# Mamba layer and exact-weight MLP on one core: the second part's first-gelu rows taken ahead, and its first block prepared beside the tail of the first part

## The chip, the cores and the metric

The kernel runs on one core of one Trainium2 chip. The metric is the device time of one execution in microseconds; three runs of the kernel before are given, and one more execution was recorded by the profiler. TensorE is called PE, VectorE DVE, ScalarE ACT, GpSimd POOL, SyncE SP. Only SP issues the DMAs that matter here.

## The reference

The input is x of shape (4, 2048, 256), float32. Two residual layers follow each other:

```
x = x + mamba(layernorm(x))          # conv of 4 taps, scan over 16 states, gate, 512 -> 256
h = silu(n @ w1 * s1) * (n @ w2 * s2)   # n = layernorm(x), 256 -> 1024, weights -1, 0, 1
h = gelu(h @ h1 * t1)                # 1024 -> 1024
h = gelu(h @ h2 * t2)                # 1024 -> 1024
x = x + (h @ w3) * s3                # 1024 -> 256
```

Since the weights of the MLP are -1, 0 or 1, the kernel may split each activation into a part rounded to float32r ("high") and the rest ("low"), and multiply both by the weights with two fast matmuls; a flag, computed early, says whether all weights have few enough bits for that. If they have, all engines take the branch `exact()`, otherwise `general()`. With the given inputs it is `exact()`.

## The kernel before, in words

**First part.** The 8192 rows are cut into 32 chunks (CHUNKS) of 256 rows. A chunk passes through stages norm, front, scan, post and mlp, and one body of the program (`bodies`, `stages`) works on several chunks at once: the scan of chunk c, beside it post of c-1 and the four quarters of mlp of c-1 to c-4. Tables PE_AT, DVE_AT, ACT_AT, POOL_AT and SP_AT say at which step of a body each engine does a piece. The mlp stage ends with h1: PE writes a pair of its output rows into one of three shared PSUM banks (L1380), ACT copies them to the tile z_out (two buffers, L775), and SP stores them to the DRAM tensor z_scratch (L549). The next job may use the bank when ACT has taken it. ACT waits before it fills a z_out buffer until the store of what was in it has landed. `ending` (L407) runs the four bodies that are left after the last scan: post of chunk 31 and the last mlp quarters. In it PE does the h1 matmuls (L1380) and the w1/w2 matmuls (L1369; jobs ug0 to ug7 of a chunk, one bank each). ACT takes the tanh of each ug job (L917), DVE gates it with two instructions (L1089, L1093) and so frees the bank, and after two of them ACT rounds (L924) and POOL subtracts (L761).

**Second part, `exact()`.** Each engine first waits in `pass_a_over` (L498) for all stores of the first part. Then come 16 blocks (CB) of 512 rows. Of a block, SP loads z from z_scratch in two DMAs of 1 MB to zb (two buffers, `load_z`, L619); ACT takes gelu of its 8 rows (`first`, L973) into the 4-deep ring wide; DVE splits each row into act_high and act_low (`split_first`, two instructions, L1173 and L1175); PE multiplies by h2 in 8 jobs of 16 matmuls (`second_layer`, L1415), each job into one of 8 banks; ACT takes the second gelu from the bank, into wide again (`second`, L980); DVE splits that row into act2_high and act2_low (`split_second`, L1173 and L1175 too); and PE multiplies by w3 in 64 matmuls (`last_layer`, L1427). `last_layer` of block b-1 stands after three h2 jobs of block b (W3_AFTER). DVE scales the result, adds x1 and so ends the block (`finish`, L1193 and L1199), and SP stores it.

The order on ACT is second(b, o), first(b+1, o) for o from 0 to 7. On DVE it is finish(b-1), then split_second(b, o), split_first(b+1, o). The split of the second gelu of row 0 waits until last_layer(b-1) has read act2. PE starts block b when all its 8 first rows are split. The first block has no such preparation in front of it: its load, its 8 gelus and its 8 splits all come after `pass_a_over`.

Of the kernel before, what the change touches and what calls it, by code (L numbers as in the profile page):

```python
# [38 lines left out]
def program(nc, x, w_in, conv_w, conv_b, w_x, w_dt, b_dt, a_log, d_skip, w_out,  # L39
# [25 lines left out]
    with ExitStack() as ctx:  # L65
# [37 lines left out]

        w_out_sb = sb("w_out_sb", [P, ET, DIM], where=a_only)
# [18 lines left out]
        dt = sb("dt", [P, 2, ET, T], where=a_only)  # L123
        u = sb("u", [P, ET, T], where=a_only)
        b_row = sb("b_row", [P, 2, QUARTER, T], where=a_only)
        b_first = sb("b_first", [P, NS], where=a_only)
        ub = sb("ub", [P, 2, ET, T], where=a_only)
        h = sb("h", [P, 2, ET, T], where=a_only)
# [33 lines left out]
        zb = sb("zb", [P, 2, KH, TB], where=b_only)  # L162
        wide = sb("wide", [P, WIDE, TB], where=b_only)
        xr = sb("xr", [P, 2, NTB, DIM], where=b_only)
# [6 lines left out]
        act_high = sb("act_high", [P, 2, KH, TB], F32R, where=b_only)  # L171
        act_low = sb("act_low", [P, 2, KH, TB], F32R, where=b_only)
# [245 lines left out]
        z_in = [sem(f"z_in{n}") for n in range(2)]  # L418
        xr_in = [sem(f"xr_in{n}") for n in range(2)]
        gelu1_ready = sem("gelu1_ready")  # L420
        high_ready = sem("high_ready")
        rows_split = sem("rows_split")
# [6 lines left out]
        W3_AFTER = 3  # L429

# [8 lines left out]

        def first_row(blk, o):  # L440
            return o if blk == 0 else KH + 2 * KH * (blk - 1) + 2 * o + 1

        def second_row(blk, o):
            return KH + 2 * KH * blk + (2 * o if blk < CB - 1 else o)
# [74 lines left out]
        def _(sp):  # L519
# [67 lines left out]
            for c in range(CHUNKS):  # L587
                to_norm, to_front, to_post, to_mlp = stages(c)
                for n in range(NS):
                    if n == SP_AT["x"] and to_norm is not None:  # L590
                        load_x(to_norm)
                    if n == SP_AT["write_b"] and to_front is not None:
                        write_b(to_front)
                    for quarter in (2, 3):
                        if n == SP_AT["b"][quarter]:
                            read_b(c, quarter)
                    for quarter in (0, 1):
                        if n == SP_AT["b"][quarter] and to_front is not None:
                            read_b(to_front, quarter)
                    if to_post is not None:  # L600
                        post(to_post, n)
                    for k in reversed(range(MLP_BODIES)):
                        if to_mlp[k] is not None:
                            mlp(to_mlp[k], NS * k + n)
                    if c == CHUNKS - 1 and n == 2:
                        sp.wait_ge(u_ready, CHUNKS)
                        sp.wait_ge(job_full, filled["acc1", CHUNKS - 1] + 1)
                        sp.wait_ge(xn_ready, CHUNKS)
                        sp.wait_ge(b_written, 32 * CHUNKS)
                        for name, src in (("h2", h2), ("w3", w3)):  # L610
                            sp.dma_start(again[name][:], src.rearrange("(k p) n -> p k n", p=P)).then_inc(late_in, 16)
            ending(post, mlp, NS)
            pass_a_over(sp)

            def exact():
                def load_z(blk):
                    after(sp, gelu1_ready, KH * (blk - 1))
                    for half in range(2):
                        sp.dma_start(zb[:, blk % 2, :, half * T:(half + 1) * T], z_dram[2 * blk + half]).then_inc(z_in[blk % 2], 16)  # L619

                def load_rows(blk):
                    after(sp, out_e_ready, blk - 1)
                    sp.dma_start(xr[:, blk % 2], x1_rows_b[:, blk]).then_inc(xr_in[blk % 2], 16)

                load_z(0)
                load_z(1)
                load_rows(0)
                load_rows(1)
                for blk in range(CB):
                    if blk + 2 < CB:  # L630
                        load_z(blk + 2)
                    sp.wait_ge(out_e_ready, blk + 1)
                    sp.dma_start(out_rows[:, blk], out_e[:, blk % 2]).then_inc(out_e_stored[blk % 2], 16)
                    if blk + 2 < CB:
                        load_rows(blk + 2)
                for slot in range(2):
                    sp.wait_ge(out_e_stored[slot], 8 * CB)

            def general():
# [17 lines left out]

                for name, src in (("w1", w1), ("w2", w2), ("h1", h1), ("h2", h2), ("w3", w3)):
                    sp.dma_start(whole_w[name][:], src.rearrange("(k p) n -> p k n", p=P)).then_inc(whole_in, 16)
# [109 lines left out]
        def _(act):  # L769
# [31 lines left out]
            def with_logs(to_front, to_norm, to_mlp):  # L801
# [12 lines left out]
                nc.scalar.preload_act_table_set("exp_and_others")  # L814
# [151 lines left out]
            ending(post, mlp, ACT_STEPS)  # L966

            def exact():
                def first(blk, o):
                    row = first_row(blk, o)  # L970
                    after(act, rows_split, row - WIDE + 1)
                    act.wait_ge(z_in[blk % 2], 32 * (blk // 2 + 1))
                    nc.scalar.activation(wide[:, row % WIDE], zb[:, blk % 2, o], ACT.Gelu, scale=scales[:, 2, o:o + 1]).then_inc(gelu1_ready, 1)  # L973

                def second(blk, o):
                    row = second_row(blk, o)
                    job = ("h2", blk, o)
                    after(act, rows_split, row - WIDE + 1)
# [52 lines left out]
        def _(dve):  # L1031
# [137 lines left out]
            ending(post, mlp, DVE_STEPS)  # L1169

            def exact():
                def split(row, blk, high, low, first_in_layer):
                    nc.vector.tensor_copy(high, wide[:, row % WIDE]).then_inc(high_ready, 1)  # L1173
                    dve.wait_ge(high_ready, row + 1)
                    nc.vector.tensor_tensor(low, wide[:, row % WIDE], high.bitcast(F32), ALU.subtract).then_inc(rows_split, 1)  # L1175

                def split_first(blk, o):
                    dve.wait_ge(gelu1_ready, KH * blk + o + 1)
                    if o == 0 and blk >= 2:
                        dve.wait_ge(e_full, e_place["h2", blk - 2, KH - 1] + 1)  # L1180
                    split(first_row(blk, o), blk, act_high[:, blk % 2, o], act_low[:, blk % 2, o], o == 0)

                def split_second(blk, o):
                    e_taken(dve, ("h2", blk, o))
                    if o == 0 and blk >= 1:
                        dve.wait_ge(e_full, e_place["out", blk - 1, NTB // 2 - 1] + 1)
                    split(second_row(blk, o), blk, act2_high[:, o], act2_low[:, o], o == 0)
# [75 lines left out]
        def _(pe):  # L1263
# [139 lines left out]
            def exact():  # L1403
                def free(job):
                    k = e_place[job]
                    after(pe, e_free[k % E_RING], k // E_RING)
                    return e_bank(job)

                def second_layer(blk, o):
                    into = free(("h2", blk, o))  # L1410
                    if o == 0:
                        pe.wait_ge(rows_split, first_row(blk, KH - 1) + 1)
                    for k in range(KH):
                        for part in (act_high, act_low):
                            last = nc.tensor.matmul(into, rounded["h2"][:, k, o * P:(o + 1) * P], part[:, blk % 2, k],  # L1415
                                                    start=(k == 0 and part is act_high), stop=(k == KH - 1 and part is act_low))
                    last.then_inc(e_full, 1)

                def last_layer(blk):
                    pe.wait_ge(rows_split, second_row(blk, KH - 1) + 1)  # L1420
# [10 lines left out]
                pass_a_over(pe)  # L1431
# [96 lines left out]
```

## Time and profile before

| | us |
|---|---|
| median of 3 runs (lowest, highest) | 3020.08 (3018.89, 3022.86) |
| the profiled execution, its own time | 3020.71 |
| its span, first to last instruction | 3018.9 |
| PE busy | 2677.9 (89%) |
| DVE busy | 2488.2 (82%) |
| ACT busy | 1831.0 (61%) |
| POOL busy | 1847.4 (61%) |

The profiled execution takes 1.8 us more than its span, and 0.6 us more than the median. The first part fills the span to about 2316 us, the second the 703 us that follow. Engines are named with the source line (L1415 is line 1415). "idle before" names the instruction that ended an idle stretch. PEclk is the granted clock of TensorE as a share of full speed; full speed is 2.4 GHz, and the other level is 1.2 GHz.

### The profile page before, as it was taken

The numbers are of one execution on the slowest core, as the hardware profiler recorded it, in microseconds if no ns is written. First come the engines' busy times: TensorE is split into PE (matmuls) and PEld (weight loads), VectorE is DVE, ScalarE is ACT, GpSimd is POOL, SyncE is SP. The second block draws the span as 40 slices with busy tenths as digits, with TensorE's granted clock in tenths as the row PEclk, the third lists the DMA queues.
The fourth block names the chain that finished last, engine by engine and source line by source line (L and its number), as shares of the span: only waits on it lengthen the run. The fifth ranks groups of instructions, "written<-read, shape, count | busy, mean of one in ns | idle before, by whom it ended". The sixth has DMA issues, their size and how long they took to land. (4 is left out here: it accounts for less than half of the span.)

```text
span 3018.9 us, 49123 instructions
## 1 busy us (share of the span) xinstructions
PE 2677.9 (89%) x17026; PEld 2350.8 (78%) x17026; DVE 2488.2 (82%) x3488; ACT 1831.0 (61%) x3488; POOL 1847.4 (61%) x1549
## 2 busy tenths in 40 slices
PE   5578999999999989999999989999876999999998
PEld 4457888888888878888888888888766787778777
DVE  4999999999999999999999999999962443454434
ACT  4667777777777777777777777777653222222221
POOL 3688888888888888888888888888841000000000
PEclk8799999999999999999999999999988999999999
DMA  6011111211212112211211112121213121222210
GB/s 212 22 50 47 54 54 58 71 61 54 70 55 61 54 54 60 68 61 54 71 54 61 54 54 65 63 61 55 95 66 125 60 82 44 84 84 84 76 51 29
DMA packets 130155, 198.78 MB, mean 66 GB/s; under 512 B 16368, under 2 KB 93296, under 8 KB 129904
## 3 DMA queue, kind: packets, MB, share of 16 engines
q1 hardware_dynamic: 129904, 195.57, 20.7%
q8 instruction: 140, 2.29, 0.3%
q14 instruction: 111, 0.91, 0.1%
HBM read 144.68 MB, written 50.86 MB: 65 GB/s over the span
## 5 line engine op out<-in xcount | busy, mean ns | idle before, releaser
L1107 DVE TENSOR_TENSOR_SCAN h<-banks,ub 128x512 f32<-128x512 f32 x1024 | 1192.1, 1205 | 42.2 <-POOL ub L738 28.9
L738 POOL TENSOR_TENSOR ub<-u,b_row 128x1020 f32<-128x1020 f32 x512 | 1214.0, 2371 | 0.3 <-issue 0.2
L1392 PE MATMUL banks<-ident,h 128*128 128x128 f32 x4096 | 608.8, 280 | 206.0 <-DVE acc L1120 195.4
L954 ACT ACTIVATE banks<-dt,neg_a 128x510 f32<-128x510 f32 x1024 | 683.8, 681 | 142.7 <-DVE h L1107 142.6
L1120 DVE SCALAR_TENSOR_TENSOR acc<-banks,c_tok,acc 128x512 f32<-128x512 f32 x1024 | 714.1, 736 | 5.8 <-PE banks L1392 4.8
L1392 PEld LDWEIGHTS banks<-ident,h 128*128 128x128 f32 x4096 | 473.9, 143 | 294.5 <-issue 126.7
L1380 PE MATMUL banks<-act_high,h_rounded 128*128 128x256 f32 x2048 | 533.3, 297 | 0.0
L1380 PE MATMUL banks<-act_low,h_rounded 128*128 128x256 f32 x2048 | 506.5, 283 | 0.0
L1415 PE MATMUL banks<-act_high,h_rounded 128*128 128x512 f32 x1024 | 419.3, 409 | 71.1 <-DVE act_low L1175 71.1
L1415 PE MATMUL banks<-act_low,h_rounded 128*128 128x512 f32 x1024 | 415.8, 406 | 0.0
L1380 PEld LDWEIGHTS banks<-act_low,h_rounded 128*128 128x128 f32 x2048 | 393.8, 192 | 0.0
L1380 PEld LDWEIGHTS banks<-act_high,h_rounded 128*128 128x128 f32 x2048 | 392.1, 191 | 0.0
L980 ACT ACTIVATE wide<-banks,scales 128x512 f32<-128x512 f32 x128 | 88.1, 689 | 484.9 <-PE banks L1415 292.6
L1415 PEld LDWEIGHTS banks<-act_high,h_rounded 128*128 128x128 f32 x1024 | 203.7, 199 | 120.7 <-issue 77.1
L1369 PE MATMUL banks<-xT_high,w_rounded 128*128 128x256 f32 x1024 | 272.0, 299 | 10.1 <-ACT z_out L775 9.1
L1193 DVE TENSOR_TENSOR prod_e<-banks,s_row 128x512 f32<-128x512 f32 x32 | 22.1, 692 | 312.6 <-PE banks L1427 312.6
L761 POOL TENSOR_TENSOR act_low<-wide,act_high 128x512 fp32r<-128x512 f32 x128 | 165.1, 1290 | 160.6 <-ACT act_high L924 160.6
L1369 PE MATMUL banks<-xT_low,w_rounded 128*128 128x256 f32 x1024 | 255.3, 282 | 0.0
L1303 PE MATMUL banks<-xp,conv_diag 128*128 128x256 f32 x1024 | 243.1, 380 | 0.0
L1415 PEld LDWEIGHTS banks<-act_low,h_rounded 128*128 128x128 f32 x1024 | 203.6, 199 | 43.1
L737 POOL TENSOR_TENSOR ub<-b_u,enter 128x4 f32<-128x4 f32 x512 | 104.8, 205 | 182.4 <-DVE h L1107 174.1
L1369 PEld LDWEIGHTS banks<-xT_high,w_rounded 128*128 128x128 f32 x1024 | 195.0, 190 | 17.4 <-ACT z_out L775 9.3
(111 smaller groups left out, 4257.0 us busy)
## 6 DMA issues: line engine op xcount, KB each, us to landing
b_row<-b_scratch SPq DMA_DIRECT2D x128, 512.0 KB, 3.9
z_scratch<-z_out SPq DMA_DIRECT2D x128, 256.0 KB, 5.0
zb<-z_scratch SPq DMA_DIRECT2D x32, 1024.0 KB, 9.0
x_sb<-in_x SPq DMA_DIRECT2D x32, 256.0 KB, 5.4
x_res<-in_x SPq DMA_DIRECT2D x32, 256.0 KB, 4.5
h_full<-in_h SPq DMA_DIRECT2D x2, 4096.0 KB, 17.9
x_scratch<-x_sb SPq DMA_DIRECT2D x32, 256.0 KB, 2.2
xr<-x_scratch SPq DMA_DIRECT2D x16, 512.0 KB, 5.8
```

The lines of the kernel that those rows point to most:

```text
L737: nc.gpsimd.tensor_tensor(ub[:, n % 2, :, 0], b_u[:, n], enter[:, n], ALU.add).then_inc(ub_ready, 1)
L738: nc.gpsimd.tensor_tensor(ub[:, n % 2, :, 1:], u[:, :, 1:], b_row[:, n // QUARTER % 2, n % QUARTER:n % QUARTER + 1, 1:].to_broadcast([P, E ...
L761: nc.gpsimd.tensor_tensor(act1_low[:, c % 2, 2 * p:2 * p + 2], wide1[:, p % 2], act1_high[:, c % 2, 2 * p:2 * p + 2].bitcast(F32), ALU.sub ...
L954: nc.scalar.activation(decay_half(k)[:, :, 1:], dt[:, par, 2 * i:2 * i + 2, 1:], ACT.Exp, scale=neg_a[:, n:n + 1]).then_inc(decay_ready, 1)
L980: nc.scalar.activation(wide[:, row % WIDE], e_bank(job), ACT.Gelu, scale=scales[:, 3, o:o + 1]).then_inc(e_free[e_place[job] % E_RING], 1)
L1107: nc.vector.tensor_tensor_scan(h[:, n % 2, 2 * i:2 * i + 2].rearrange("p e t -> p (e t)"), banks[:, k % DECAYS, :], ub[:, n % 2, 2 * i:2 * ...
L1120: nc.vector.scalar_tensor_tensor(out=acc[:, par, q], in0=turned[q], scalar=c_tok[:, par, q, n:n + 1], in1=acc[:, par, q], op0=ALU.mult, op ...
L1303: last = nc.tensor.matmul(into[:, i * T:(i + 1) * T], conv_diag[:, e, tap], xp[:, e, tap:tap + T], start=(tap == 0), stop=(tap == TAPS - 1))
L1369: last = nc.tensor.matmul(into[:, j * T:(j + 1) * T], weights[:, d, o * P:(o + 1) * P], rows[:, d], start=(d == 0 and rows is xT_high), st ...
L1380: last = nc.tensor.matmul(into[:, i * T:(i + 1) * T], rounded["h1"][:, k, o * P:(o + 1) * P], rows[:, c % 2, k], start=(k == 0 and rows is ...
L1392: last = nc.tensor.transpose(turned[q][:, e * P:(e + 1) * P], h[:, n % 2, e, q * P:(q + 1) * P], ident[:])
L1415: last = nc.tensor.matmul(into, rounded["h2"][:, k, o * P:(o + 1) * P], part[:, blk % 2, k], start=(k == 0 and part is act_high), stop=(k ...
```

## The change

- The tiles. `zb` is replaced by three tiles zl[0..2], taken in turn by block number modulo 3. The gelu is computed in place, and act_low[0..2] are in the same memory as zl[0..2]: DVE rounds the row to act_high (two tiles, block number modulo 2) and subtracts in place. The ring wide is left to the second gelu alone. zl[0] lies on memory of the scan's tiles, which are free when the last scan is over; zl[1] and zl[2] lie on the rounded weights of the first part, which are free when its last matmul is over. For that, five tiles of the scan (dt, u, b_row, ub, h) are declared earlier.
- The order of the second part. On ACT first(b+1, o) stands ahead of second(b, o), on DVE split_first(b+1, o) ahead of split_second(b, o), and finish(b-1) comes behind split_second(b, 3) instead of at the head of the block. One semaphore for all splits becomes one for the first and one for the second rows.
- The first block. SP issues the load of zl[0] ahead of `ending`, once the scan is over. ACT takes its 8 gelus and DVE its 8 splits in body 33 (the second of the four bodies of `ending`), at each fourth step of ACT's 32 and each sixth of DVE's 48. ACT loads the function table of gelu at its last change of table in the first part, instead of at the head of the second.
- The waits. PE no longer waits in `pass_a_over`, but for the rounded late weights (h2, w3) and the last scan's sums; where block 0 writes into one of the three shared banks, it waits for that bank. SP loads zl[1] and zl[2] after the last matmul of the first part. Later loads wait for the last h2 job of the block three before.

```diff
-        def ending(post, mlp, steps):
+        def ending(post, mlp, steps, first_rows=lambda c, n: None):
...
                     if to_post is not None:
                         post(to_post, n)
+                    first_rows(c, n)
...
+        FIRST_ROWS = [(CHUNKS + 1, 4 * o) for o in range(KH)]
...
+            def load_z(blk):
+                for slot in range(2):
+                    sp.wait_ge(z_stored[slot], 16 * PAIRS // 2 * 2 * (blk + 1))
+                for half in range(2):
+                    sp.dma_start(zl[blk % 3][:, :, half * T:(half + 1) * T], z_dram[2 * blk + half]).then_inc(z_in[blk % 3], 16)
+
+            sp.wait_ge(scan_done, 2 * NS * CHUNKS)
+            for q in range(NT):
+                sp.wait_ge(turn_full[q], NS * CHUNKS)
+            sp.wait_ge(carry_ready, NS * CHUNKS - 2)
+            load_z(0)
             ending(post, mlp, NS)
-            pass_a_over(sp)
...
-                load_z(0)
+                wait_full(sp, f"h{PAIRS - 1}", CHUNKS - 1)
                 load_z(1)
+                load_z(2)
+                pass_a_over(sp)
...
                 for blk in range(CB):
-                    if blk + 2 < CB:
-                        load_z(blk + 2)
+                    if blk + 3 < CB:
+                        sp.wait_ge(e_full, e_place["h2", blk, KH - 1] + 1)
+                        load_z(blk + 3)
...
-                    with_logs(None, None, c)
+                    with_logs(None, None, c, "gelu_and_others" if c == CHUNKS - 1 else "exp_and_others")
...
+            def first(blk, o):
+                act.wait_ge(z_in[blk % 3], 32 * (blk // 3 + 1))
+                nc.scalar.activation(zl[blk % 3][:, o], zl[blk % 3][:, o], ACT.Gelu, scale=scales[:, 2, o:o + 1]).then_inc(gelu1_ready, 1)
...
                 pass_a_over(act)
-                for o in range(KH):
-                    first(0, o)
                 for blk in range(CB):
                     for o in range(KH):
-                        second(blk, o)
                         if blk + 1 < CB:
                             first(blk + 1, o)
+                        second(blk, o)
...
+            def split_first(blk, o):
+                rows, high = zl[blk % 3][:, o], act_high[blk % 2][:, o]
+                dve.wait_ge(gelu1_ready, KH * blk + o + 1)
+                if o == 0 and blk >= 2:
+                    dve.wait_ge(e_full, e_place["h2", blk - 2, KH - 1] + 1)
+                nc.vector.tensor_copy(high, rows).then_inc(high1_ready, 1)
+                dve.wait_ge(high1_ready, KH * blk + o + 1)
+                nc.vector.tensor_tensor(act_low[blk % 3][:, o], rows, high.bitcast(F32), ALU.subtract).then_inc(split1, 1)
...
                 pass_a_over(dve)
-                for o in range(KH):
-                    split_first(0, o)
                 for blk in range(CB):
-                    if blk >= 1:
-                        finish(blk - 1)
                     for o in range(KH):
-                        split_second(blk, o)
                         if blk + 1 < CB:
                             split_first(blk + 1, o)
+                        split_second(blk, o)
+                        if o == W3_AFTER and blk >= 1:
+                            finish(blk - 1)
                 finish(CB - 1)
...
                     into = free(("h2", blk, o))
                     if o == 0:
-                        pe.wait_ge(rows_split, first_row(blk, KH - 1) + 1)
+                        pe.wait_ge(split1, KH * (blk + 1))
...
-                pass_a_over(pe)
+                pe.wait_ge(rounded_late, 10)
+                for q in range(NT):
+                    pe.wait_ge(y_added[q], NS * CHUNKS)
                 for blk in range(CB):
```

How the change moves the instructions is shown at three places.

**DVE, where block 1 ends and block 2 begins.** act and wide are first and second rows, the tiles called act2 belong to the second rows, prod_e and out_e to `finish`. Before:

```order
L1173 CAST act2_high<-wide 128x512
L1175 TENSOR_TENSOR act2_low<-wide,act2_high 128x512
L1173 CAST act_high<-wide 128x512
L1175 TENSOR_TENSOR act_low<-wide,act_high 128x512
L1193 TENSOR_TENSOR prod_e<-banks,s3_row 128x512 x2
L1199 TENSOR_TENSOR out_e<-prod_e,xr 128x1024
```

After the change, the same place two blocks on (zl1 is the block's own row 7, zl2 the next block's row 0):

```order
L1194 CAST act_high0<-zl1 128x512
L1196 TENSOR_TENSOR act_low1<-zl1,act_high0 128x512
L1210 CAST act2_high<-wide 128x512
L1212 TENSOR_TENSOR act2_low<-wide,act2_high 128x512
L1194 CAST act_high1<-zl2 128x512
L1196 TENSOR_TENSOR act_low2<-zl2,act_high1 128x512
```

The last first-row split, which PE waits for, now stands ahead of the last second-row split, and `finish` is gone from the head of the block.

**SP, round the load of zl[0].** z_scratch<-z_out are stores of h1 pairs, with the bank whose release each waits for. Before, from the second pair of chunk 28 on:

```order
L549 DMA z_scratch<-z_out 128x512 [waits bank_free0] x2
L549 DMA z_scratch<-z_out 128x512 [waits bank_free2]
L530 DMA x1_scratch<-x1_sb 128x2x256 [waits x1_ready]
L549 DMA z_scratch<-z_out 128x512 [waits bank_free0]
L549 DMA z_scratch<-z_out 128x512 [waits bank_free1] x2
```

After the change:

```order
L556 DMA z_scratch<-z_out 128x512 [waits bank_free0]
L624 DMA zl0<-z_scratch 128x8x256 [waits carry_ready,z_stored0,turn_full1,z_stored1,turn_full0,scan_done]
L624 DMA zl0<-z_scratch 128x8x256
L556 DMA z_scratch<-z_out 128x512 [waits bank_free0]
L556 DMA z_scratch<-z_out 128x512 [waits bank_free2]
L537 DMA x1_scratch<-x1_sb 128x2x256 [waits x1_ready]
```

The stores of the third and fourth pair of chunk 28 now stand behind the wait for the end of the scan and behind 2 MB of load.

**ACT, in body 33, where the ug jobs of chunk 31 are taken.** tanh1 is the tanh of a ug job. Before:

```order
L917 ACTIVATE tanh1<-banks,half_s1 128x256
L775 ACTIVATE z_out<-banks 128x512
L917 ACTIVATE tanh1<-banks,half_s1 128x256 x2
L924 ACTIVATE act1_high<-wide1 128x512
L917 ACTIVATE tanh1<-banks,half_s1 128x256 x2
L924 ACTIVATE act1_high<-wide1 128x512
```

After the change:

```order
L987 ACTIVATE zl0<-zl0,scales 128x512
L935 ACTIVATE tanh1<-banks,half_s1 128x256
L793 ACTIVATE z_out<-banks 128x512
L935 ACTIVATE tanh1<-banks,half_s1 128x256
L987 ACTIVATE zl0<-zl0,scales 128x512
L935 ACTIVATE tanh1<-banks,half_s1 128x256
L942 ACTIVATE act1_high<-wide1 128x512
L935 ACTIVATE tanh1<-banks,half_s1 128x256
L987 ACTIVATE zl0<-zl0,scales 128x512
```

Gelus of block 0 stand between the tanh instructions; on DVE the splits stand between the gates in the same way.

## Rows read from the trace of the kernel before

**Rows 1.** The page: engine totals.
```profile
PE 2677.9 (89%) x17026; PEld 2350.8 (78%) x17026; DVE 2488.2 (82%) x3488; ACT 1831.0 (61%) x3488; POOL 1847.4 (61%) x1549
```
**Rows 2.** Chain that ended last, second part: start us, us, engine, output, line, count.
```profile
2339.11 32.08 PE banks L1415 x128
...
2374.35 12.78 PE banks L1415 x48
2387.13 7.67 PE banks L1427 x64
2394.80 18.17 PE banks L1415 x80
...
2499.60 13.89 PE banks L1415 x48
...
2963.15 12.59 PE banks L1415 x48
```
**Rows 3.** Waits from 2300 us on: in total, times, longest us.
```profile
PE banks L1415 <- DVE act_low L1175: 71.1, 16, 23.4
```
**Rows 4.** PE instructions in order of time, at the first boundary after block 1.
```profile
2412.57 0.39 PE L1415 MATMUL banks<-act_low,h_rounded 128*128 128x512 f32 x1
2416.14 0.47 PE L1415 MATMUL banks<-act_high,h_rounded 128*128 128x512 f32 x1 [3.18 <-DVE act_low L1175]
```
**Rows 5.** Busy time by stretch: stretch, length, engines' busy us, PEclk, DMA share, GB/s.
```profile
2416.10:2428.90 12.80, 12.76 (x50) 10.43 (x51) 0.00 (x0) 2.60 (x4) 0.00 (x0) 0.87 0.00 0
2436.50:2454.70 18.20, 18.20 (x81) 14.74 (x79) 16.42 (x30) 6.84 (x10) 0.00 (x0) 1.00 0.55 173
2256.00:2316.00 60.00, 59.64 (x484) 58.81 (x482) 16.58 (x38) 22.37 (x42) 11.41 (x10) 1.00 0.15 54
```
**Rows 6.** DVE in order of time, behind the last layer of block 1.
```profile
2436.68 0.69 DVE L1193 TENSOR_TENSOR prod_e<-banks,s_row 128x512 f32<-128x512 f32 x1 [3.22 <-PE banks L1427]
...
2438.55 0.42 DVE L1173 CAST act_high<-wide 128x512 fp32r<-128x512 f32 x1
...
2451.92 0.43 DVE L1173 CAST act_high<-wide 128x512 fp32r<-128x512 f32 x1 [0.53 <-ACT wide L980]
...
2457.07 0.69 DVE L1175 TENSOR_TENSOR act_low<-wide,act_high 128x512 fp32r<-128x512 f32 x1
```
**Rows 7.** ACT in order of time: second gelu of row 6 in the same block.
```profile
2451.20 0.69 ACT L980 ACTIVATE wide<-banks,scales 128x512 f32<-128x512 f32 x1 [2.33 <-PE banks L1415]
```
**Rows 8.** Chain that ended last, from the first part to the second.
```profile
2295.58 20.17 PE banks L1380 x168
...
2318.54 0.02 SPq L503
...
2320.01 8.12 DMA zb<-z_scratch
...
2338.28 0.70 DVE act_low L1175
```
**Rows 9.** The same chain earlier, in the tail of the first part.
```profile
2244.64 1.23 PE banks L1392 x8
...
2254.49 0.97 PE banks L1369 x8
...
2291.74 2.88 PE banks L1380 x24
```
**Rows 10.** DMA issues from 2200 to 2345 us: count, KB, median us to landing.
```profile
zb<-z_scratch SPq DMA_DIRECT2D x6, 1024.0 KB, 8.1
z_scratch<-z_out SPq DMA_DIRECT2D x16, 256.0 KB, 2.1
xr<-x_scratch SPq DMA_DIRECT2D x2, 512.0 KB, 9.6
```
**Rows 11.** ACT in the tail, in order of time: z_out of the first pair of chunk 29.
```profile
2253.19 0.60 ACT L775 ACTIVATE z_out<-banks 128x512 f32<-128x512 f32 x1 [3.42 <-PE banks L1380]
```
**Rows 12.** DVE in the tail, in order of time: gate of ug4 of chunk 31.
```profile
2290.83 0.48 DVE L1093 SCALAR_TENSOR_TENSOR wide<-banks,gate_scale,tanh 128x256 f32<-128x256 f32 x1
```

More of the change, by code:

```diff
@@ L102, in program @@
         ssm = sb("ssm", [P, 2, T], where=a_only)
+        dt = sb("dt", [P, 2, ET, T], where=a_only)
+        u = sb("u", [P, ET, T], where=a_only)
+        b_row = sb("b_row", [P, 2, QUARTER, T], where=a_only)
+        ub = sb("ub", [P, 2, ET, T], where=a_only)
+        h = sb("h", [P, 2, ET, T], where=a_only)
         w_out_sb = sb("w_out_sb", [P, ET, DIM], where=a_only)
@@ L161, in program @@
         WIDE = 4
-        zb = sb("zb", [P, 2, KH, TB], where=b_only)
-        wide = sb("wide", [P, WIDE, TB], where=b_only)
-        xr = sb("xr", [P, 2, NTB, DIM], where=b_only)
+        zl, act_low, act_high = [None] * 3, [None] * 3, [None] * 2
+        with ExitStack() as as_loaded:
+            zl[1] = sb("zl1", [P, KH, TB], where=as_loaded)
+        act_low[1] = sb("act_low1", [P, KH, TB], F32R, where=b_only)
+        act_high[1] = sb("act_high1", [P, KH, TB], F32R, where=b_only)
+        with ExitStack() as as_loaded:
+            zl[2] = sb("zl2", [P, KH, TB], where=as_loaded)
+        act_low[2] = sb("act_low2", [P, KH, TB], F32R, where=b_only)
         again = {}
@@ L415, in ending @@
                         post(to_post, n)
-        z_in = [sem(f"z_in{n}") for n in range(2)]
+                    first_rows(c, n)
+        z_in = [sem(f"z_in{n}") for n in range(3)]
         xr_in = [sem(f"xr_in{n}") for n in range(2)]
         gelu1_ready = sem("gelu1_ready")
-        high_ready = sem("high_ready")
-        rows_split = sem("rows_split")
+        high1_ready = sem("high1_ready")
+        split1 = sem("split1")
+        high2_ready = sem("high2_ready")
+        split2 = sem("split2")
         e_full = sem("e_full")
@@ L813, in with_logs @@
                     exp_rows2(to_mlp)
-                nc.scalar.preload_act_table_set("exp_and_others")
+                nc.scalar.preload_act_table_set(then)
             def norm(c, n):
@@ L965, in _, with first_rows @@
             bodies(norm, front, scan, post, mlp, lambda: None, ACT_STEPS)
-            ending(post, mlp, ACT_STEPS)
-            def exact():
[L969 to L973, printed above, removed]
+            def first(blk, o):
+                act.wait_ge(z_in[blk % 3], 32 * (blk // 3 + 1))
+                nc.scalar.activation(zl[blk % 3][:, o], zl[blk % 3][:, o], ACT.Gelu, scale=scales[:, 2, o:o + 1]).then_inc(gelu1_ready, 1)
+            def first_rows(c, n):
+                if (c, n) in FIRST_ROWS:
+                    first(0, FIRST_ROWS.index((c, n)))
+            ending(post, mlp, ACT_STEPS, first_rows)
+            def exact():
                 def second(blk, o):
-                    row = second_row(blk, o)
+                    row = KH * blk + o
                     job = ("h2", blk, o)
-                    after(act, rows_split, row - WIDE + 1)
+                    after(act, split2, row - WIDE + 1)
                     act.wait_ge(e_full, e_place[job] + 1)
@@ L1168, in _, with first_rows @@
             bodies(norm, lambda c, n: None, scan, post, mlp, make_diagonals, DVE_STEPS)
-            ending(post, mlp, DVE_STEPS)
-            def exact():
[L1172 to L1181, printed above, removed]
+            def split_first(blk, o):
[6 more added lines that the diff above has]
+                nc.vector.tensor_tensor(act_low[blk % 3][:, o], rows, high.bitcast(F32), ALU.subtract).then_inc(split1, 1)
+            def first_rows(c, n):
+                if n % 3 == 0 and (c, 2 * n // 3) in FIRST_ROWS:
+                    split_first(0, FIRST_ROWS.index((c, 2 * n // 3)))
+            ending(post, mlp, DVE_STEPS, first_rows)
+            def exact():
                 def split_second(blk, o):
+                    row = KH * blk + o
                     e_taken(dve, ("h2", blk, o))
@@ L1411, in second_layer @@
                     if o == 0:
-                        pe.wait_ge(rows_split, first_row(blk, KH - 1) + 1)
+                        pe.wait_ge(split1, KH * (blk + 1))
                     for k in range(KH):
-                        for part in (act_high, act_low):
-                            last = nc.tensor.matmul(into, rounded["h2"][:, k, o * P:(o + 1) * P], part[:, blk % 2, k],
-                                                    start=(k == 0 and part is act_high), stop=(k == KH - 1 and part is act_low))
+                        for i, part in enumerate((act_high[blk % 2], act_low[blk % 3])):
+                            last = nc.tensor.matmul(into, rounded["h2"][:, k, o * P:(o + 1) * P], part[:, k],
+                                                    start=(k + i == 0), stop=(k == KH - 1 and i == 1))
                     last.then_inc(e_full, 1)
                 def last_layer(blk):
-                    pe.wait_ge(rows_split, second_row(blk, KH - 1) + 1)
+                    pe.wait_ge(split2, KH * (blk + 1))
                     for j in range(NTB // 2):
```

32 lines of the change are left out of this document (15 added, 17 removed).

## Prediction

> **What bounds the kernel now.** I read the page first: PE is busy 89% of the span [rows 1]. Then the chain of waits that ended last over the second part, since the change lies there. From 2339 us on it is almost all PE, in a pattern of three pieces per block: 48 matmuls of h2, 64 of the last layer, 80 of h2 [rows 2]. Between two blocks the chain leaves PE and runs over ACT and DVE. The waits say how much: PE waits 71.1 us for DVE's split in 16 places, the longest 23.4 [rows 3]. So the other 15 are (71.1 - 23.4) / 15 = 3.18 us each, and the instructions in order of time show one of them [rows 4]. Last, busy time by stretch, with PE's granted clock [rows 5]: right behind a boundary it is 0.87 over 12.8 us, later in the block 1.00, with DVE and DMA far busier. So the loss is not contention. In the chain the first 48 matmuls take 12.6 to 13.9 us, the other 80 only 18.17, which is 0.227 us each [rows 2]. At that pace 48 take 10.90. A boundary costs its 3.18 us, and then 1.7 to 3.0 us at 1.2 GHz.
>
> Why PE waits there: the last h2 job of block b ends, ACT takes the second gelu of row 7 and only behind it the first gelu of the next block's row 7; DVE splits them in the same order, two splits of 1.07 us. That pace is from DVE's rows: twelve splits between 2438.55 and 2451.39, the start of the 0.53 us of idle [rows 6].
>
> **Boundaries.** The change puts row 7 of the next block ahead of the second gelu of row 7. It then depends on no bank of the last job, only on ACT and DVE being in time. I work that out in the block whose last layer ends at 2436.57 (DVE's wait ends at 2436.68) [rows 6], h2 then ending at 2454.74, 18.17 later. DVE cannot split second row 0 until the last layer ends. From 2436.68 it has second row 0, then first and second of rows 1, 2 and 3: 7 splits, 7.5 us, to 2444.2. Then `finish`: before it took from 2436.68 to 2438.55 with one of its two multiplies already done, so 1.87 + 0.7 = 2.6 us, to 2446.8. Rows 4 and 5 are 4 splits, to 2451.1, and first row 6 ends at 2452.1. Second row 6 is ready by then (ACT starts it at 2451.20, when PE has finished job 6) [rows 7]. It and first row 7 are 2 splits, to 2454.3. PE can use them 0.15 later: before, the split ending at 2338.98 let it start at 2339.11 [rows 2, 8]. That is 2454.4, and the next matmul is due at about 2454.6. So it fits, with only **0.2 to 0.3 us to spare**. I take the gap as zero, and with it the slow stretch, since every slow stretch follows a gap in these rows. ACT has 16 gelus of about 0.7 us in a block, 11 us, and is not near its limit.
>
> Per block then: 128 x 0.2271 + 7.67 = 36.74 us. Before, 14 blocks from 2374.35 to 2963.15 took 42.06 each [rows 2]. Saved: 14 x 5.32 = 74.4, plus the gap before 2374.35 (32.08 after 2339.11 is 2371.19, so 3.2) and the slow start at 2963.15 (12.59 - 10.90 = 1.7). Together **-79.3**. Bounds: -79.3 with no gap, and nothing gained if each boundary keeps a gap; the arithmetic above is nearest to no gap.
>
> **Between the parts.** PE ends the first part at 2315.75 [rows 8], then waits 23.4 us [rows 3]: for SP to store, branch and load (DMA 8.12 us) [rows 8], then for gelu and 8 splits. After the change nothing of this is in front of PE but its own branch on the flag. The trace shows no such branch of PE with work before and behind it. The nearest row is SP's: from the end of its wait at 2318.54 to its load in flight at 2320.01, 1.5 us [rows 8], DMA issue included. Below that the bound is 0, if PE's sequencer runs ahead of its array. I take the middle, 0.7: **-22.7**. Block 0 took 32.08 us for 128 matmuls [rows 2]; at 0.2271 they are 29.07, and if so short a gap leaves the clock up, **-3.0**.
>
> Block 1 must be ready when block 0 ends, 29.07 us after its start. Before, the load was under way 4.3 us after PE's last matmul, 2.1 of them for the last store to land [rows 8, 10], for which zl[1] does not wait; so it is asked for at 2.2 and lands 8.1 later. ACT's first gelu takes 0.7, and DVE has 7 pairs of splits and one more, 16 us: 27.0 against 0.7 + 29.07 = 29.8. It fits, and the end of the block is then as tight as the others: 0, at worst 2 us and a slow stretch of 3.
>
> **Tail of the first part.** Two places can cost. The first is SP's queue. SP now waits for the last scan's transposes (2245.87) [rows 9], issues 2 MB, and only then stores the third pair of chunk 28, which before was stored at once, at about 2240.5. ACT's z_out of chunk 29's first pair, at 2253.19 [rows 11], needs that buffer back. The load lands 8.1 us after issue, and a 512 KB load behind 4 MB took 9.6 where a store alone takes 2.1 [rows 10]. So the store lands at about 2255.5 and ACT starts 2.3 us late. It used to end at 2253.79, and PE's next ug job began at 2254.49 [rows 9, 11], so 0.7 is slack: **+1.6**. Bounds: 0, if the store passes the load, and 4.6, if the wait also brings a slow stretch of 3.0. The Trainium skill (DMA: Bandwidth & Descriptors, "Queues, rings and completion order") says that each DMA engine takes one queue's descriptors in ring order. By that rule the store cannot pass the load and the term is the full one, not 0; the 9.6 against 2.1 agrees.
>
> The second place is body 33. 8 gelus of 0.7 on ACT and 8 splits of 1.07 on DVE are added. Most fall where both are idle. Three do not: during PE's six ug jobs in a row, which need banks that DVE's gates free. Gate of ug4 ended at 2291.31 [rows 12], and PE took that bank at 2291.74 [rows 9]. With one split before it, and the tanh behind an added gelu, it ends at about 2292.5: PE starts 0.9 late. The later splits delay only what has slack (the next h1 matmuls depend on earlier banks): **+0.9**. Bounds 0 and 2.5, which is all three splits less 0.7 of slack. The change of table costs the same there as before, for the gelu table only replaces the other.
>
> **What else moves.** POOL has nothing added. The end is as before: the last block has no first rows, and its last splits, last layer and store are unchanged. More DMA is not issued, only earlier. That SBUF tiles lie elsewhere costs nothing that a row shows.
>
> **Sum.** -79.3 - 22.7 - 3.0 + 1.6 + 0.9 = -102.5. The profiled execution took 3020.7, so 2918.2; against the median, 0.6 lower, 2917.6. I give **2918**. Its bounds: best, no branch gap and no tail cost, 2915; worst, 0.7 + 3.0 + 1.6 + 5 more, 2928.
>
> **Rivals.**
> - *DVE comes late at the boundaries.* The margin is 0.2 to 0.3 us, so waits between instructions of 0.05 us over 15 splits would use it up. Then a gap of about 0.7 stays at 15 boundaries and, if a short gap is enough to drop the clock, 2.1 with it: 15 x 2.8 = 42, so **2960**. For it: the narrow margin. Against it: the paces I used are start to start, with such waits inside.
> - *The clock falls without a gap.* If the slow stretch belongs to the block's beginning, where only PE works, and not to the wait, only the gaps go: 15 x 2.1 + 3 = 35 comes back, **2953**. Against it: the same matmuls run at 1.00 later, and PE ran 60 us without a break at 1.00 [rows 5].
> - *The change prepares block 0 no earlier* (the load or the splits come last in the tail). Then up to 23 us stay, 2941. Against it: landing by 2256, gelus from 2275, last split by 2299, need at 2318.
> - *Slower: an unbroken load brings a lower granted clock.* PE would run 588 us (16 x 36.74) nearly without a rest. At a clock of r the second part would take 588 / r; it decides against the change if 588 x (1/r - 1) is over 102, so below r = 0.85. At 0.80, 147 us, **3065**. For it: a stretch at 0.87 exists. Against it: the 60 us at 1.00 on full load [rows 5], and that all slow stretches here follow rest, not work.
>
> **Chances.** Forecast 0.70; DVE late 0.12; clock falls anyway 0.09; block 0 late 0.06; slower 0.02; and 0.01 that what I took as hidden cancels all the gain. A measurement of this kernel can tell 0.2%, 6 us, from no change. So faster 0.97, same 0.01, slower 0.02. The range 2912 to 2954 takes in the forecast with its bounds, the block 0 case and the clock case, and leaves out DVE late, the cancelled gain and slower, 0.15 in all; below 2915 I add 3 for block-to-block variation.
>
> **What would show it.** In the profile after: no PE idle of 3 us at L1415's counterpart, blocks of 36.7 us, 48 matmuls in 10.9; PE idle under 1.5 us between the parts, and the first h2 matmul about 2318.9; block 0 in 29.1; ug0 of chunk 30 about 1.6 later and h1 of chunk 30 another 0.9. I am wrong if PE still waits for DVE at the boundaries, if PEclk is below 1.00 in blocks without a wait, or if the tail grows by more than 5 us.

## The result and the profile after

| | before | after |
|---|---|---|
| median, us (lowest, highest) | 3021.01 (3018.89, 3022.86), 4 runs | 2918.55 (2917.72, 2919.70), 4 runs |
| profiled execution, us | 3020.71 | 2918.62 |
| span, us | 3018.9 | 2916.8 |

The changed kernel takes 0.9665 of the time before (95% interval 0.9653 to 0.9678), against the forecast of 2918. The ratio stands as recorded; the quotient of the two medians is 0.9661. Four runs of the kernel before count here, since one more was made beside the changed kernel.

The chain that ended last in the changed kernel, second part (start us, us, engine, output, line, count; L1441 is h2, L1453 the last layer), answers to [rows 2] and [rows 8]:

```profile
2300.44 20.16 PE banks L1403 x168
2320.60 39.92 PE banks L1441 x176
2360.52 7.67 PE banks L1453 x64
2368.19 29.07 PE banks L1441 x128
2397.27 7.67 PE banks L1453 x64
...
2875.16 7.67 PE banks L1453 x64
2882.83 18.17 PE banks L1441 x80
...
2903.02 7.95 PE banks L1453 x64
```

From 2300 us to 2901 the chain never leaves PE. The h1 matmuls of the first part (L1403) run into block 0 without a gap at 2320.60, and one block follows the other every 36.75 us (2397.27 - 2360.52; 42.06 before). The waits of PE from 2300 us on have shrunk from the 71.1 us of [rows 3] to one at the very end:

```profile
PE banks L1453 <- DVE act_low L1212: 2.0, 1, 2.0
```

Busy time by stretch (length, busy us of PE, PE's weight loads, DVE, ACT and POOL, PEclk, DMA share, GB/s) answers to [rows 5]: 540 us with PE busy throughout and the clock at full speed in all of it. The first row is the stretch in which 7.4 MB (205 GB/s for 36 us) are loaded beside the work: z of blocks 1, 2 and 3, 2 MB each, and 1 MB of x1.

```profile
2324.00:2360.00 36.00, 36.00 (x161) 29.80 (x160) 17.78 (x34) 13.27 (x21) 0.00 (x0) 1.00 0.64 205
2360.00:2900.00 540.00, 540.00 (x2832) 466.10 (x2831) 277.48 (x505) 147.22 (x226) 0.00 (x0) 1.00 0.24 76
```

DVE in order of time, in the block whose last layer ends at 2404.94, answers to [rows 6]. L1194 and L1196 are the split of a first row, L1210 of a second:

```profile
2421.47 0.42 DVE L1194 CAST act_high<-zl 128x512 fp32r<-128x512 f32 x1
2421.93 0.69 DVE L1196 TENSOR_TENSOR act_low<-zl,act_high 128x512 fp32r<-128x512 f32 x1
2423.92 0.43 DVE L1210 CAST act_high<-wide 128x512 fp32r<-128x512 f32 x1 [1.30 <-ACT wide L1001]
```

h2 of this block ends at 2404.94 + 18.17 = 2423.11. The last first-row split ends at 2422.62, PE's next block begins at 2422.94 without a break, and only after h2's end does the second row 7 follow, at 2423.92, off PE's path. The split ends 17.68 us behind the last layer; the prediction had 2454.3 - 2436.6 = 17.7.

The tail of the first part got longer. In the chain before block 0:

```profile
2244.96 1.24 PE banks L1415 x8
...
2246.33 0.62 SPq L624
...
2246.99 0.68 SPq L624
...
2247.72 8.42 DMA z_scratch<-z_out
...
2256.16 0.61 ACT z_out L793
...
2256.81 1.70 PE banks L1392 x8
2258.51 1.71 PE banks L1403 x8
```

SP issues the two loads of zl[0] right after the last scan's transposes (2246.20), and the store behind them takes 8.42 us to land, where the median store took 2.1 [rows 10]. ACT waits for it, PE waits for ACT, and the next 8 + 8 matmuls take 1.7 us each instead of 0.96: they run at the lower clock (PEclk is 0.57 from 2256.81 to 2260.20). From the end of the transposes to the last h1 matmul it is 74.4 us (2246.20 to 2320.60), before 69.9 (2245.87 to 2315.75) [rows 8, 9].

### The profile page after: what moved, and what is told of

The parts are those of the page before. It is cut to its first block and busy times, and to the rows that moved or that the text cites. A ratio compares the mean times of both kernels' runs of the same rounds, so it can differ in the third digit from the quotient of the medians.

```text
span 2916.8 us, 49010 instructions
## 1 busy us (share of the span) xinstructions
PE 2639.8 (91%) x17026; PEld 2325.9 (80%) x17026; DVE 2488.0 (85%) x3488; ACT 1823.7 (63%) x3487; POOL 1846.8 (63%) x1549
## 5 line engine op out<-in xcount | busy, mean ns | idle before, releaser
L1403 PE MATMUL banks<-act_high,h_rounded 128*128 128x256 f32 x2048 | 534.5, 297 | 0.7 <-DVE wide L1112 0.7
L1403 PE MATMUL banks<-act_low,h_rounded 128*128 128x256 f32 x2048 | 507.3, 284 | 0.0
L1441 PE MATMUL banks<-act_low,h_rounded 128*128 128x512 f32 x1024 | 398.9, 390 | 0.0
L1441 PE MATMUL banks<-act_high,h_rounded 128*128 128x512 f32 x1024 | 398.8, 389 | 0.0
L1403 PEld LDWEIGHTS banks<-act_low,h_rounded 128*128 128x128 f32 x2048 | 394.5, 193 | 0.0
L1403 PEld LDWEIGHTS banks<-act_high,h_rounded 128*128 128x128 f32 x2048 | 393.3, 192 | 0.9 <-DVE wide L1112 0.9
L1210 DVE CAST act_high<-wide 128x512 fp32r<-128x512 f32 x128 | 54.1, 423 | 265.0 <-PE banks L1453 236.0
L1441 PEld LDWEIGHTS banks<-act_high,h_rounded 128*128 128x128 f32 x1024 | 192.2, 188 | 40.1
L1441 PEld LDWEIGHTS banks<-act_low,h_rounded 128*128 128x128 f32 x1024 | 192.3, 188 | 39.6
```

What stands on the lines that cost most here:

```text
L1403: last = nc.tensor.matmul(into[:, i * T:(i + 1) * T], rounded["h1"][:, k, o * P:(o + 1) * P], rows[:, c % 2, k], start=(k == 0 and rows is ...
```

## The experiments

All are measured against the kernel before in the same job. "Less" and "more" in what follows are against the changed kernel's 2918.55 us, unless said otherwise.

**1. The order of rows alone, back to what it was.** On ACT, and on DVE in the same way:

```diff
-                        if blk + 1 < CB:
-                            first(blk + 1, o)
                         second(blk, o)
+                        if blk + 1 < CB:
+                            first(blk + 1, o)
```

> The changed kernel, but in the second part ACT and DVE take each row of the present block ahead of the next block's row, as before the change; all else stays. Theory (row order alone makes the wait at the boundaries, and every wait of 3.2 us is followed by a stretch at the lower clock): 15 gaps of 3.2 us come back and 15 slow starts of 1.7 to 3.0 us with them, together 79 us: 2998 us, PEclk under 1.00 in the first 12.8 us of each block. Rival (the slow stretches went for another reason, such as finish moved or loads earlier): only the gaps return, 48 us: 2966 us. Second rival (the third z buffer or the moved finish did it, not the order): stays at 2919 us.

Measured: 3000.4 us, ratio to before 0.9935 (0.992 to 0.995), 82 us more. PE's waits, and the chain of two blocks:

```profile
PE banks L1441 <- DVE act_low L1196: 47.7, 15, 3.2
```
```profile
2354.30 12.61 PE banks L1441 x48
...
2395.92 13.91 PE banks L1441 x48
```

47.7 us of waits in 15 places, and slow starts of 12.6 to 13.9 us, as before the change. The third buffer, the place of `finish` and the weaker waits stayed changed in this kernel and prevented none of it. So the order of rows is needed for the gain, and the slow start comes and goes with the wait. Whether the order would do it alone, without the third buffer and the moved `finish`, no run here shows.

**2. The gap filled with work, in the kernel before.**

```diff
                     if o == 0:
+                        if blk >= 1:
+                            for _ in range(24):
+                                nc.tensor.matmul(into[:, 0:DIM], rounded["h2"][:, 0, 0:P], rounded["w3"][:, 0], start=True, stop=True)
                         pe.wait_ge(rows_split, first_row(blk, KH - 1) + 1)
```

> The kernel before, with 24 extra matmuls of 256 columns on constant weights put at each of the 15 boundaries, into the bank that the next job overwrites, ahead of PE's wait; the results are not used. The wait for the split stays as long (24 x 0.12 is 2.9 of its 3.2 us). Theory (PE being idle drops the clock, the gap's own length stays): blocks still 39.9 us apart, but no slow start: 32 us less than before, 2989 us. Rival (the slow start belongs to the place in the block, or follows the wait whatever PE does in it): 3020 us or a little more.

Measured: 2990.1 us, 0.9905 of before (0.989 to 0.992). PE in order of time at the boundary of [rows 4], and the stretch behind it:

```profile
2411.01 3.03 PE L1414 MATMUL banks<-w_rounded,h_rounded 128*128 128x256 f32 x24
2414.26 0.50 PE L1418 MATMUL banks<-act_high,h_rounded 128*128 128x512 f32 x1 [0.22 <-DVE act_low L1175]
```
```profile
2414.30:2427.10 12.80, 12.80 (x64) 10.90 (x65) 0.00 (x0) 2.60 (x4) 0.00 (x0) 1.00 0.00 1
```

The real work of a block is still held up as long, from 2411.2 to 2414.26. But PE is idle for only 0.22 us, PEclk is 1.00 where it was 0.87 [rows 5], and 48 matmuls take 11.2 us. Adding 360 matmuls made the kernel 29 us faster. Blocks are now 40.1 us apart, where they were 42.06 before and are 36.75 in the changed kernel. This splits a boundary's 5.3 us in two: 3.3 that stay with the wait, and 2.0 that idleness costs afterwards. Of the 3.3, about 3.1 are the wait itself. The rest is a slightly slow start at full clock: 11.17 us for 48 matmuls behind the wait, where 48 without a wait take 10.90. The prediction put all of a slow start down to the lower clock.

**3. Block 0 prepared behind the first part, as before the change.**

```diff
-            load_z(0)
             ending(post, mlp, NS)
...
                 pass_a_over(sp)
+                load_z(0)
...
                 pass_a_over(act)
+                for o in range(KH):
+                    first(0, o)
```

(and the same for `split_first` on DVE; `first_rows` is not passed to `ending`.)

> The changed kernel, but the load, the 8 gelus and the 8 splits of block 0 come after the end of the first part, as before the change; the order of the second part stays changed. Theory: a gap of 23.4 us and a slow start of 3.0 us between the parts come back, the tail loses the 4.5 us that the preparation cost it: 2918.5 + 23.4 + 3.0 - 4.5 = 2940 us. Rival (the tail's loss has another cause than the preparation): 2945 us, with PE's last h1 matmul still at 2320.

Measured: 2938.0 us, 0.973 of before (0.9715 to 0.9745), 19.4 more. The gap between the parts is back, 1.9 us shorter than before the change. Of that, 1.3 are the load of the gelu table, which in the kernel before stands on ACT behind the DMA (1.28 us at 2328.22) and is already done here. About 0.5 are SP's reading of the flag, which in the kernel before stands between its wait and the load (2318.73 to 2319.29).

```profile
PE banks L1444 <- DVE act_low L1197: 21.5, 1, 21.5
```

Block 0 and the first 48 matmuls of block 1 take 43.03 us (39.92 in the changed kernel), a slow start of 3.1. PE's first part ends at 2315.3. So 21.5 + 3.1 - 5.3 = 19.3. The sum leaves out the last layer of the last block, which took 9.41 us in this profile and 7.95 in the changed kernel's (experiment 6); the two profiled executions themselves are 21.1 us apart.

**4. SP's queue and the place of the splits, each alone and together.** SP's edit puts the load behind the two stores of chunk 28. The other puts rows 4 to 7 of block 0 into body 34, which has no ug jobs:

```diff
+            def load_first(c, n):
+                if (c, n) == (CHUNKS, 6):
...
+                    load_z(0)
...
-            ending(post, mlp, NS)
+            ending(post, mlp, NS, load_first)
```
```diff
-        FIRST_ROWS = [(CHUNKS + 1, 4 * o) for o in range(KH)]
+        FIRST_ROWS = [(CHUNKS + 1 + o // 4, 4 * (o % 4)) for o in range(KH)]
```

> The changed kernel with only SP's edit: block 0's load behind the two stores of chunk 28. Theory: the first of the two costs goes, 3.5 us: 2915 us. The stores land 2.1 us after issue and ACT's z_out of chunk 29 no longer waits for a DMA. Rival (the load delays the next stores as much): no change, 2918.5 us.

> The changed kernel with only the other edit: gelus and splits of rows 4 to 7 of block 0 in body 34. Theory: 1.1 us less, 2917.4 us; six ug jobs of chunk 31 follow each other on PE without a wait. Rival (rows in body 34 come too late for block 0): a gap between the parts, more than 2919 us.

> The changed kernel with two edits in the tail: SP loads block 0 behind the two stores of chunk 28 instead of ahead of them (body 32, behind step 5), and the gelus and splits of rows 4 to 7 of block 0 stand in body 34, which has no ug jobs. Theory (those two places cost the tail 3.5 and 1.1 us): 4.5 us less than the changed kernel, 2914 us, PE's last h1 matmul ending near 2316.1. Rival (other contention of the preparation, such as its 2 MB of DMA or ACT's gelus wherever they stand, costs it): 2917 to 2919 us.

> The kernel of tail_mended once more, on the chip of last_filled, as its partner. Theory: 2914 us, the 64 matmuls of the last layer at 9.4 or 7.95 us.

| kernel | median, us | ratio to before (interval) | transposes' end to last h1 matmul, us |
|---|---|---|---|
| before | | | 69.9 |
| block 0 late (experiment 3) | 2938.0 | 0.973 (0.9715 to 0.9745) | 68.4 |
| changed | 2918.6 | 0.9665 (0.9653 to 0.9678) | 74.4 |
| load moved | 2916.1 | 0.9653 (0.9637 to 0.9669) | 69.5 |
| rows moved | 2918.7 | 0.9665 (0.9649 to 0.9682) | 71.9 |
| both | 2914.0 and, again, 2912.8 | 0.9653 (0.964 to 0.9667), 0.9647 (0.9634 to 0.966) | 68.4 |

The last column is from the chain of each profiled execution. For both edits together it starts and ends like this:

```profile
2243.66 1.22 PE banks L1419 x8
2244.88 6.71 PE banks L1407 x56
...
2252.03 0.97 PE banks L1396 x8
...
2289.28 2.88 PE banks L1407 x24
```
```profile
2313.28 39.92 PE banks L1445 x176
```

The medians of single edits say little: the last scan ended anywhere from 2244.9 to 2248 us in these executions, before anything of the change runs, and that is as much as an edit is worth. The tail's own length says it. With both edits it is 6.0 us shorter than in the changed kernel, with the load moved alone 4.9, so the splits' place costs 1.1 (69.5 - 68.4). With the rows moved alone 3.4 are left (71.9 - 68.4). So SP's queue cost 3.4 in one execution and 4.9 in the other, where it brought a longer slow stretch. The same tail stands in four more kernels, those of experiment 5 and of experiment 1, where it is 73.2, 74.4, 74.6 and 74.7 us. With both edits the tail is as short as in the kernel of experiment 3, which prepares nothing in it (68.4), so the preparation then costs the tail nothing. It is also 1.5 shorter than before the change. The reason is a slow stretch in the profile before: its 56 h1 matmuls behind the transposes take 8.19 us at a PEclk of 0.79, here 6.71 at 1.00. PE is idle for 1.85 us ahead of those transposes before the change, and just as long in the kernel with the load moved, where the 56 take 6.72. In the medians the rows moved alone gain nothing that can be told. The ten runs with both edits, 2912.0 to 2915.9 us, all lie below the four of the changed kernel; the intervals of their ratios overlap, since they were measured in different jobs. It is the best version found: 2914.0 us.

**5. How late may DVE be?** One, two or four instructions of 0.7 us are added on DVE in each block but the last, ahead of second row 5, which work on a tile that nothing reads:

```diff
+                        if o == KH - 3 and blk + 1 < CB:
+                            for i in range(1):
+                                after(dve, padded, 1 * blk + i)
+                                nc.vector.tensor_tensor(pad[:], ..., ..., ALU.mult).then_inc(padded, 1)
                         split_second(blk, o)
```

> The changed kernel with one extra DVE instruction of 0.7 us in each block, ahead of second row 5 (a product of constants into a tile of its own, which nothing reads). The margin of the last first-row split is 0.2 to 0.3 us by my working, so PE gets a gap of about 0.4 to 0.5 us at 15 boundaries. Theory A (so short a gap leaves the clock up): 6 to 8 us more, 2926 us. Theory B (any gap drops the clock): 2.1 us more at each, 2957 us. If the margin were 0.7 us or more: 2918.5 us.

> The changed kernel with two extra DVE instructions in each block, 1.4 us, so a gap of about 1.1 to 1.2 us at 15 boundaries, 17 us. Theory (the longer the gap, the more of them drop the clock; 0.3 us never did, 2.4 us nearly always): between 2936 us, if none of the 15 drops it, and 2962 us, if all do; I expect few drops, 2936 to 2945 us.

> The same with four such DVE instructions, 2.8 us: a gap of about 2.5 us at 15 boundaries, 38 us. Theory A (a gap must be about as long as the 3.2 us of the kernel before to drop the clock): 2957 us. Theory B (2.5 us drops it too): 2.1 us more at each, 2988 us. Between them, if it drops at some boundaries only.

| added on DVE, us | median, us | ratio (interval) | PE's idle at a boundary | a block |
|---|---|---|---|---|
| 0 | 2918.6 | 0.9665 (0.9653 to 0.9678) | none | 36.75 |
| 0.7 | 2924.9 | 0.9685 (0.9669 to 0.9701) | 0.3 | 37.2 |
| 1.4 | 2936.8 | 0.9723 (0.9708 to 0.9737) | 1.0 | 38.0 |
| 2.8 | 2979.9 | 0.9867 (0.9851 to 0.9884) | 2.4 | 40.9 |

PE's waits in the three, in this order:

```profile
PE banks L1448 <- DVE act_low L1198: 3.8, 14, 0.3
```
```profile
PE banks L1448 <- DVE act_low L1198: 14.3, 14, 1.3
```
```profile
PE banks L1448 <- DVE act_low L1198: 35.7, 15, 2.5
```

The first boundary of the third kernel, and one of the others with PE behind it:

```profile
2349.71 0.47 PE L1448 MATMUL banks<-act_high,h_rounded 128*128 128x512 f32 x1 [1.49 <-DVE act_low L1198]
...
2429.96 0.77 PE L1448 MATMUL banks<-act_high,h_rounded 128*128 128x512 f32 x1 [2.44 <-DVE act_low L1198]
2430.52 0.63 PE L1448 MATMUL banks<-act_low,h_rounded 128*128 128x512 f32 x1
...
2432.65 0.57 PE L1448 MATMUL banks<-act_high,h_rounded 128*128 128x512 f32 x1
2433.07 0.40 PE L1448 MATMUL banks<-act_low,h_rounded 128*128 128x512 f32 x1
```

0.7 us of extra work cost 0.5 us per block, so the margin was 0.2 us, as worked out. It can be read directly too: in the changed kernel the split ends at 2422.62, PE can use it 0.14 later, and takes it at 2422.94. Gaps of 0.3 us, and of 1.0 (the last of those 14 is 1.3), leave the clock up: the first 48 matmuls take 11.1 to 11.2 us, and PEclk is 1.00 behind the first gap of each of the two kernels. In the kernel with 2.8 us added there are 14 gaps of 2.4 us and one, the first, of 1.5. All 14 drop the clock (12.5 to 12.7 us for 48 matmuls), for a cost of about 4.2 us each; the one of 1.5 us doesn't (11.16 us). That kernel fell nearer to theory B (2988 us) than to A (2957), so a gap needn't be as long as 3.2 us to drop the clock.

**6. The last gap.** Ahead of the last layer of the last block PE is idle for 2.0 us in all kernels. 16 extra matmuls fill it, on top of both edits of experiment 4.

> The kernel of tail_mended with 16 extra matmuls of 256 columns on constant weights (unused results) ahead of PE's wait for the last layer of the last block, where PE is idle for 2.0 us. In the profiles so far those 64 matmuls took 9.4 us in some and 7.95 in others behind the same 2.0 us of idle. Theory (a gap of 2.0 us drops the clock or not by where it falls in time, and the matmuls keep it up): the 64 take 7.7 us always, 0 to 1.5 us less than tail_mended's 2914.0, so about 2913. Rival (the slow ones have another cause, such as DVE's last splits beside them): 9.4 us still occurs, and 2914.

Measured: 2913.7 us, 0.965 of before (0.9637 to 0.9663), beside 2912.8 for its partner without them: no difference that can be told. Both profiles show the 64 matmuls at 7.95 us, so neither says whether the filler holds the clock. Over the 12 profiled executions that have this gap unfilled, they took 9.40 to 9.45 us in 7 and 7.95 in 5, with the same 2.0 us before them. So behind a gap of 2.0 us the matmuls are slow or not by something other than the gap's length. What, no run here settles.

## Why the prediction was right, and where its terms were off

- **The boundaries (-79.3).** Right in mechanism and in size. Blocks are 36.75 us apart where 36.74 was said. Undoing only the order costs 82 us (experiment 1). The wait carries a second cost, a slow stretch behind it. The prediction took that as following from the wait, and filling the gap shows it (experiment 2).
- **The margin of 0.2 to 0.3 us.** Right: 0.2 by experiment 5. The rival "DVE comes late" did not come true, but its trigger was close: 0.7 us more work on DVE is enough for a gap. Its price was wrong. It had a gap of 0.7 us bring 2.1 us of slow start with it, and gaps of 0.3 and 1.0 us brought none; that rival would have given about 2929, not 2960.
- **The clock falls without a gap.** Refuted: 540 us at 1.00 with PE busy throughout. The slower rival, a lower clock under unbroken load, falls by the same row.
- **Between the parts (-22.7 and -3.0).** The 0.7 us for PE's branch was the wrong value between its bounds: the chain shows none, its lower end. The gap saved 23.4. The slow start of block 0 went as said, and block 1 was ready in time though 5 MB were loaded beside block 0.
- **The tail, SP's queue (+1.6).** The mechanism was right to the instruction: z_out of chunk 29's first pair waits for the store behind the load. The size was not. Against the kernel before, the tail is 4.5 us longer, and 1.1 of it are the splits, so the queue's part is 3.4. Of these 2.0 are the wait: the ug job began 8.6 us behind the transposes before (2245.87 to 2254.49) and 10.6 after (2246.20 to 2256.81), since the store landed about 0.3 later than worked out. The rest, about 1.5, is the slow stretch that the wait brought. The sum left it out and had it only in the bound, so that is where the term was too small. Against the kernel with the load moved, the queue costs 4.9. That is more because the profile before has a slow stretch of 1.5 us of its own in this place (8.19 against 6.72 us for 56 matmuls), and the one with the load moved has none.
- **The tail, the splits (+0.9).** 1.1, by experiment 4.
- **The end, taken as unchanged.** It was 1.5 us shorter in this profile (9.45 us before, 7.95 after). Both values occur behind the same 2.0 us gap in kernels with the change and without it (experiment 6), so this is chance and no work of the change.
- **The sum.** Span for span: second part from its first matmul on, 679.8 before (2339.11 to 3018.9), 596.2 after, 83.6 less; gap 23.4 less; tail 4.5 more, and the last scan 0.3 later by chance: 102.2. The forecast was -102.5. It hit so closely by luck, because errors cancelled: the tail's cost was 2.0 us too low and the last scan came 0.3 later, while the branch (0.7) and the end (1.5) made up for it.

## What to carry to other kernels

When PE waits for the next block's operands, look whether another engine's queue puts work that depends on the current block's last result ahead of them; swapping the two rows was worth 82 us of 3020 here and added no instruction. Price such a wait as gap plus the slow stretch behind it, and if the gap can't be removed, fill it with harmless matmuls. When a load is pulled forward into a busy queue, check which buffers are waiting for a store that now stands behind it, count the slow stretch that such a wait can bring, and look whether the stretch from which you measure is itself slowed.

## What the runs showed of the hardware that I had not expected

- Idle time of PE and the clock: gaps of 0.3 us (14), of 1.0 to 1.3 us (14) and one of 1.5 us did not drop it. Behind gaps of 2.0 us the matmuls were slow in 7 of 12, behind 2.4 us in 14 of 14, behind 3.2 us in all 15, both before the change and with the order swapped back. All are gaps in a long stretch in which PE is otherwise busy.
- PE passed from the first part into the branch `exact()` without any idle time, though its program loads the flag and compares it there: the last h1 matmul starts at 2320.32 and the first of h2 at 2320.44, as close as two h1 matmuls.
- One of the eight DVE subtractions of block 0, with both inputs in SBUF, took 1.66 us instead of 0.69, beside a POOL instruction of the same kind. In the changed kernel, DVE and POOL in order of time:

```profile
2299.53 1.66 DVE L1196 TENSOR_TENSOR act_low<-zl,act_high 128x512 fp32r<-128x512 f32 x1
```
```profile
2299.12 1.53 POOL L779 TENSOR_TENSOR act_low<-wide,act_high 128x512 fp32r<-128x512 f32 x1 [2.67 <-ACT act_high L942]
```

DVE's instruction ends 0.5 us after POOL's, a little less than its own length. The Trainium skill (SBUF — State Buffer, "Who interferes with whom") says that a DVE instruction with two SBUF inputs contends with a GpSimd instruction that reads SBUF, for a read interface that the two share. The rows agree, though they are one case. With rows 4 to 7 moved to body 34, none of the eight subtractions starts beside a POOL instruction, and all took 0.69. The prediction had priced all splits at 1.07 us and missed this. It cost nothing here, since PE had other work.
